# AdaLN block of a delta-rule mixer and a three-matrix FFN on eight cores: the last tile turned on TensorE, its last passes in halves, the plan of the order chosen among eight

## What is computed

```python
mod = (_silu(c) @ wmod).reshape(8, 6, 1, -1)
sa, ca, ga, sb, cb, gb = (mod[:, 0], ..., mod[:, 5])
ga, gb = (both with their sign kept and their size raised to at least 0.25)
h = _layernorm(x) * (1 + ca) + sa
x = x + ga * attn(h)
h = _layernorm(x) * (1 + cb) + sb
x = x + gb * jnp.tanh(h @ weight @ aux_weight1 @ aux_weight2 + bias)
# attn: q, k, v = silu(causal conv of 4 taps of x @ Wq, Wk, Wv), 4 heads of 256
#   o = chunkwise delta rule(l2norm q, l2norm k, v, beta), chunks of 32
#   mix = p0 * v + p1 * conv3(v) + p2 * conv31(v), p a softmax over three
#   o = rms_norm(g * o + (1 - g) * mix); return o @ Wo
```

## Time and profile before

| | |
|---|---|
| median of 3 timed runs | 774.94 us (773.45 to 778.86) |
| the profiled execution | 777.23 us |
| its span on the slowest core (core 5) | 775.7 us |
| spans of the eight cores | 760.5 to 775.7 us |
| busy: TensorE, VectorE, ScalarE, GpSimd | 706.0 (91%), 581.7 (75%), 419.6 (54%), 192.4 us (25%) |
| chain that ended last, by engine | TensorE 70%, DMA 14%, VectorE 5%, issue 4% |
| matmuls of TensorE | 5888 |

### The profile page before, as it was taken

How to read it: one execution, slowest core, us unless ns; L and a number is a source line. 1 busy time by engine, 2 the same in 40 slices (tenths; PEclk the granted TensorE clock), 3 DMA queues, 4 the chain that set the end, 5 groups by cost and what they waited for, 6 DMA issues and landing times.

```text
span 775.7 us, 17911 instructions; the slowest of 8 cores (760.5 to 775.7 us)
## 1 busy us (share of the span) xinstructions
PE 706.0 (91%) x5888; PEld 485.6 (63%) x5888; DVE 581.7 (75%) x1554; ACT 419.6 (54%) x915; POOL 192.4 (25%) x167
## 2 busy tenths in 40 slices
PE   3679997998897987899999999999999989999996
PEld 1234474576685876678778778788887844444432
DVE  3554755477879778887887798798798777787885
ACT  1132463466657655785766657686675632254422
POOL 1000000025406333462332242133234103040110
PEclk9999996699999999999999999999999999999999
DMA  8999898561453344335423505223249597829944
GB/s 225 320 321 320 252 279 182 183 90 56 75 70 106 47 89 114 45 69 86 94 42 58 122 15 83 80 73 97 71 55 174 155 193 189 238 62 239 216 88 150
DMA packets 121488, 105.15 MB, mean 136 GB/s; under 512 B 68926, under 2 KB 102261, under 8 KB 121014
## 3 DMA queue, kind: packets, MB, share of 16 engines
q1 hardware_dynamic: 98150, 89.29, 44.7%
q0 software_dynamic: 20944, 10.53, 11.5%
q10 hardware_dynamic: 2304, 4.20, 1.5%
HBM read 79.38 MB, written 18.89 MB: 127 GB/s over the span
## 4 chain that ended last, share of the span: by engine, by line
PE 70%; DMA 14%; DVE 5%; issue 4%; SPq 3%; ACT 2%; POOL 1%; ACTq 0%; DVEq 0%; POOLq 0%
PE ps L930 19%; PE ps L976 10%; PE ps L1613 7%; PE ps L1559 5%; DMA z_k<-w 3%; PE ps L1331 3%; PE ps L1295 2%; PE ps L705 2%; DMA w1t_sb<-wk 2%; PE ps L1227 2%; PE ps L1442 2%; PE ps L1421 2%; DMA w_d<-w_sb 2%; PE ps L1390 2%; PE ps L649 1%
## 5 line engine op out<-in xcount | busy, mean ns | idle before, releaser
L930 PE MATMUL ps<-h,wq_sb 128*128 128x256 bf16 x512 | 72.0, 288 | 3.4 <-DVE S L1450 3.0
L930 PE MATMUL ps<-h,wk_sb 128*128 128x256 bf16 x512 | 69.1, 276 | 1.3 <-ACT h L904 0.7
L930 PE MATMUL ps<-h,wv_sb 128*128 128x256 bf16 x512 | 65.9, 272 | 0.0
L930 PEld LDWEIGHTS ps<-h,wq_sb 128*128 128x128 bf16 x512 | 51.6, 103 | 16.9 <-issue 7.1
L1613 PE MATMUL ps<-wq_sb,h 128*128 128x512 bf16 x256 | 60.7, 380 | 0.3 <-DVE xf L1574 0.3
L1279 POOL TENSOR_SCALAR vbs<-vtm,gt 128x256 bf16<-128x256 bf16 x64 | 60.9, 963 | 0.0
L1559 PE MATMUL ps<-wk_sb,ofm 128*128 128x512 bf16 x256 | 57.4, 379 | 3.2 <-DMA ofm<-o_d 3.1
L1273 POOL TENSOR_TENSOR eb<-vtm 128x1024 bf16<-128x1024 bf16 x16 | 34.5, 2157 | 99.1 <-ACT vtm L391 37.8
L930 PEld LDWEIGHTS ps<-h,wk_sb 128*128 128x128 bf16 x512 | 48.7, 99 | 11.2 <-issue 3.2
L1118 DVE TENSOR_TENSOR E<-NN,cb_sb 128x512 bf16<-128x512 bf16 x112 | 48.9, 452 | 5.0 <-PE ps L1172 3.8
L807 PE MATMUL ps<-w1t_sb,w_sb 128*128 128x512 bf16 x128 | 34.2, 435 | 19.8 <-DVE w1t_sb L552 15.4
(11 more groups left out here) (240 smaller groups left out, 1821.5 us busy)
## 6 DMA issues: line engine op xcount, KB each, us to landing
xs<-x SPq DMA_DIRECT2D x16, 512.0 KB, 5.6
mst<-wmod POOLq DMA_DIRECT2D x16, 512.0 KB, 5.9
xf<-x SPq DMA_DIRECT2D x16, 512.0 KB, 4.6
out<-xf SPq DMA_DIRECT2D x16, 512.0 KB, 2.9
w1t_sb<-wk SPq DMA_DIRECT2D x8, 512.0 KB, 10.6
w1t_sb<-wq SPq DMA_DIRECT2D x8, 512.0 KB, 7.3
w1t_sb<-wv SPq DMA_DIRECT2D x8, 512.0 KB, 5.4
o_d<-ob ACTq DMA_DIRECT2D x16, 256.0 KB, 2.2
```

The costliest lines, as they stand in the source:

```text
L930: (lambda e, g=g: e.matmul(bk[:, 256 * i:256 * (i + 1)], wt[:, 2048 * p + 256 * g + 128 * i:2048 * p + 256 * g + 128 * (i + 1)], hv[:, 256 ...
```

## The change

Five edits.

- weave plans eight times, each time with the tails of the plan before. It keeps the tails that gave the plan whose last store ends first by the planner's own costs, and lays out all engines by them. These are the tails of the first plan, so the order used is the second plan; before it was the third.
- The planner's cost of an SP or ACT DMA is 480 ns for each DMA of a step and no longer 60 for the step; for POOL it is 600 for each.
- A Share gives banks only if `keep` more would still be free: two for most, one for ring_x, none for ring, ring_l and ring_r.
- The last tile's normed x is no longer turned by a DMA. Eight transposes on TensorE in two banks (new line L1620) and two casts into h2 replace it.
- The last tile's multiply, add and store (new lines L1670, L1672, L1675) work on two halves of 512 columns. For this th is posted half by half.

```diff
     def ready(self, n):
-        return self.pool.ready(n) if n <= self.cap else None
+        return self.pool.ready(n) if n <= self.cap and self.pool.ready(n + self.keep) is not None else None
...
-            return Step({eng: (emits, 600.0 if eng == "gpsimd" else 60.0)}, [t for t in after if t is not None],
+            return Step({eng: (emits, (600.0 if eng == "gpsimd" else 480.0) * len(emits))}, [t for t in after if t is not None],
...
-            tails = None
-            for turn in range(2):
-                tails = layout(None, None, tails).tails_of()
+            if not plan:
+                tails, found = None, []
+                for turn in range(8):
+                    trial = layout(None, None, tails)
+                    found.append((max(trial.board["out", n].at for n in range(NC)), turn, tails))
+                    tails = trial.tails_of()
+                plan.append(min(found)[2])
+            tails = plan[0]
...
+                    else:
+                        evs = []
+                        for half in range(2):
+                            mm = yield st("tensor", [t], lambda bk, half=half: [
+                                (lambda e, g=g: e.transpose(bview(bk)[:, 128 * (g % 4):128 * (g % 4 + 1)],
+                                                            xn2[n % 3][:, 128 * g:128 * (g + 1)], eye))
+                                for g in range(4 * half, 4 * half + 4)], 4 * mmw(128), ring=ring_o)
+                            ev = yield evac([mm] + fr, h2[n % 3][:, 512 * half:512 * (half + 1)],
+                                            bview(mm.banks[0])[:, 0:512], 512)
+                            ring_o.give(mm.banks[0], ev)
+                            evs.append(ev)
+                        post("h2", n, evs)
...
+                    for part in (slice(0, 1024),) if n < NC - 1 else (slice(0, 512), slice(512, 1024)):
+                        half_ths = []
+                        for half in range(part.start // 512, part.stop // 512):
+                            half_ths.append((yield Need(("th", n, half))))
+                        width = part.stop - part.start
+                        t3 = yield st("vector", half_ths + [rp], [lambda e: e.tensor_tensor(
+                            th[n % 2][:, part], th[n % 2][:, part], gb_rep[:, part], ALU.mult)], 1.15 * width)
+                        t4 = yield st("vector", [t3] + xts, [lambda e: e.tensor_tensor(
+                            x[:, part], x[:, part], th[n % 2][:, part], ALU.add)], 1.15 * width)
+                        t = yield dma("sync", s_out[n % NXF], [t4], [
+                            lambda e, n=n: e.dma_start(out_r[n, :, part], x[:, part])], 500.0 * width)
```

30 lines of the change are left out of this document (14 added, 16 removed).

## The result

The changed kernel takes 785.25 us (median of 13 runs, 778.93 to 825.87), the kernel before 775.6 beside it. The ratio is 1.0102, with a 95% interval of 1.0076 to 1.0127: about 8 us slower, where 2.3 us faster was predicted. The medians take in every run, the ratios only those in which the cores of one die did not run at a lower clock than the others. The profiled execution took 783.8 us, 1.45 us under the median.

A forecast was written before the change was run, and what follows sets the result against it. TensorE was taken as the bound, winnable only in idle and low-clock time. The terms -5.2 - 1.3 + 4.5 - 0.3 + 0 gave -2.3 us on the median of 774.9: 772.6 us, range 762 to 784.

The forecast's parts named there:

- What bounds the kernel: Whole kernel: TensorE is the bound, so a new order can win back only its idle time and time at low clock.
- Part 1, the gap at 116 us: TensorE gap before z_q's convolution shrinks from 4.0 to about 2.1 us and the half-clock spell goes: -5.2 us.
- My sign of full clock from 120 to 130 on every core: After the gap near 116 us: granted clock of 1.0 from 120 to 130 us on every core.
- Part 2, the hand-over: After v's last convolution, near 622 us: less TensorE waiting on ofm loads, -1.3 us, bounds 0 and -3.1.
- Part 3, the late gb_rep: Last stage: gb_rep lands 50.1 us after the last convolution and holds up TensorE; +4.5 us, bounds 0 and +13.
- the stall of 3.5 us in front of tile 3: Last product, second half of tile 3: TensorE stops 3.5 us for a PSUM bank held because gb_rep is late.
- the row store: Store of the last gb row ahead of gb_rep: given 2.9 us to land, the nearest row being out<-xf.
- Part 4, the tail: Last tile: TensorE resumes some 1.5 us later, halved passes and store win it back; sum -0.3 us, bounds -1.8 and +1.5.
- Part 5, the rest: Rest of the order, TensorE's 25.6 us idle from 150 to 400 us: taken as 0, bounds -10 and +5.6.
- third rival: Tiles 0 to 3 and x loads of tiles 6 to 9: late gb_rep breaks the slot chain, 783 to 787 us; chance 0.20.
- low-clock rival: Near 116 us: the gap of 2.1 us or L649's four-byte matmuls still bring low clock, 776 to 778 us; chance 0.12.
- clearly better: Low-clock spell goes on every core, two POOL multiplies meet VectorE work they do not hold: 760 to 767 us; chance 0.20.

The follow-up runs named there:

- e15: Changed kernel, order unchanged, with the four gb-row loads cut to an eighth and the gb matmuls and row passes behind them cut too; ratio 1.0017 to the kernel before.
- e9: Changed kernel, second plan, with the last block's first v convolution planned only once the four gb rows are; ratio 1.0294 to the kernel before.
- e1: Kernel before with only the last tile's two edits (turned on TensorE, last passes in halves), old planner and third plan; ratio 1.0005 to the kernel before.
- e6: Changed kernel with the shares' keep undone (keep=0), all else as changed; ratio 0.9863 to the kernel before.
- e14: Kernel before with only the 480 ns DMA cost and the second plan, no keep and no tail edits; ratio 0.9980 to the kernel before.
- e19: e14, order unchanged, with the gb load that POOL issues at 573 us cut to an eighth; ratio 0.9850 to the kernel before, three runs.

## Why the prediction was wrong, point by point

**What bounds the kernel**: right. What was won or lost is idle time on TensorE and matmuls that ran slower, in about equal parts on the mean core.

**Part 1, the gap at 116 us (-5.2)**: right in mechanism and place. z_q's convolution follows the projections without a wait, and the largest wait near there is 2.08 us on the eight cores (3.98 in the earlier trace rows). TensorE and VectorE on core 3:

```profile
118.59 1.03 PE L939 MATMUL ps<-h,wq_sb 128*128 128x256 bf16 x8
119.46 1.04 PE L985 MATMUL ps<-z_q,cdiag 128*128 128x256 bf16 x8
120.34 0.34 PE L1083 MATMUL ps<-cb_sb,sqb 128*128 128x1 bf16 x8
```

The clock on that core from 120 to 130 us is 0.98; half clock came later and shorter (0.51 from 130 to 140, a stretch that I had not named). My sign of full clock from 120 to 130 on every core failed on cores 1 and 4 (0.66 and 0.50). Over 112 to 150 us the clock was 0.64 to 0.91 on the eight cores (mean 0.82) and is 0.78 to 1.00 (mean 0.88). The first wv projections start at 140.7 us at the latest (148.06 in the earlier trace rows) and at 138.7 on the mean core (141.4 before). Where the last convolution ends, the slowest core was 7.3 us ahead, the mean core 2.9. The sum had one slip: a gap cut from 4.0 to 2.1 us with the same matmuls around it is 1.9 won and not 1.3. No run took this edit alone, so its worth in the total is read from the trace and not shown by an experiment.

**Part 2, the hand-over (-1.3)**: wrong in sign. The waits on ofm in sum are 5.2 us on core 3 (3.1 in the earlier trace rows), and 3.7 on the mean core against 1.7. The step that failed is that I counted the matmuls ahead of each wait and took the landing of the loads as fixed. It is not: in the new order a gb load lies beside them. I had the place of the gb groups in hand, in part 3, and used it for their matmuls and row stores only, not for the 512 KB loads that they need.

**Part 3, the late gb_rep (+4.5)**: right in when, wrong in what it does. SP's, VectorE's and TensorE's rows:

```profile
668.54 0.35 SPq L1544 DMA_DIRECT2D gb_rep<-row_d  x1
...
670.41 2.80 PE L1635 MATMUL ps<-wq_sb,h 128*128 128x512 bf16 x8
673.47 1.90 PE L1635 MATMUL ps<-wq_sb,h 128*128 128x512 bf16 x8
...
673.79 1.23 DVE L1670 TENSOR_TENSOR th<-th,gb_rep 128x1024 f32<-128x1024 f32 x1 [1.62 <-DMA gb_rep<-row_d]
```

gb_rep is used 58.9 us behind the last convolution (I had 50.1 for its landing), and the multiply waits for it. But TensorE, held up in the recurrence and on ofm, comes to these products later than I had reckoned, so the stall of 3.5 us in front of tile 3 is not there: L1635 runs on. The +4.5 was charged to a place that costs nothing. e15 shows that the work of the gb steps costs nothing, e9 that this order pays more when they are forced ahead. One term was sized badly: the row store, which I gave 2.9 us to land, is issued at 667.31, and gb_rep is issued 1.2 us behind it. What made gb_rep late is TensorE's own lateness: the last group for it starts 47.6 us behind the last convolution, and I had 39.1.

**Part 4, the tail (-0.3)**: right. Core 3:

```profile
771.31 0.62 PE L1620 MATMUL ps<-cb_sb,xn 128*128 128x128 bf16 x8
...
772.75 1.89 PE L1635 MATMUL ps<-wq_sb,h 128*128 128x512 bf16 x8 [0.82 <-ACT h L392]
...
778.69 0.69 DVE L1672 TENSOR_TENSOR xf<-xf,th 128x512 f32<-128x512 f32 x1
```

0.62 and 0.82 are lost (1.5 foreseen). Behind the last matmul 4.7 us are left and were 6.4, a gain of 1.7 (1.8 foreseen). e1 measured the sum as nothing.

**Part 5, the rest (0)**: this term failed, though the idle time from 150 to 400 us moved little (25.6 to 23.6 us on the slowest cores). It was the largest unknown and I gave it no sign and its bounds only from POOL's multiply. That one cost less than before: three of four held VectorE, for 3.05, 4.00 and 4.73 us, and TensorE behind them for 0.96, 2.74 and 3.26, where I had counted 10. The fourth held one of 8 columns (L1064) for 1.55, which takes about 0.16 elsewhere. As for the rule that I had cited from the Trainium skill ("SBUF — State Buffer", "Who interferes with whom"), the trace agrees for three of them, L1323, L1127 and L1064: they have two inputs in SBUF and end with the multiply or up to 0.6 us behind it. The one of 3.05 (L1264) reads a single tile and a column of scalars, and it stretched too. But the new loss was no compute instruction at all. It was the transposition at 350 us, 0.43%. The first wv matmul of a block shows it on the mean core: the new order is 8.5 us ahead at the fourth block (338.0 against 346.4) and 4.9 at the fifth (406.2 against 411.1). So the order had won something in this stretch, and the meeting took it back. I had looked at every engine's order and at SP's, and not at which transfer of POOL's queue is in the air when SP issues a transposition.

**The rivals.** The time, 785, lies in the interval of the third rival (783 to 787), and its mechanism did not happen: no store or load chain broke. A hit of that kind is worth nothing for the next kernel. The range ended at 784 because that rival was the only way to lose that I had priced. The low-clock rival was wrong; "clearly better" came true only where keep is taken out (e6, and e14 with one load cut, e19).

The sum as it came, on the slowest core and read from the traces: 7.3 us ahead at the last convolution, 13.4 behind after it, and 6.1 us more of span. On the mean core it is 2.9, 12.2 and 9.3.

## What to carry to other kernels

When a change moves instructions, list for each transfer that an engine waits for which other transfers are in flight beside it on any queue, in the old order and the new. The transpositions and the 2 MB load here were issued within 0.3 to 1.0 us of the load that they met, the store of o_d 4.3 us behind it, and twice such meetings decided 1.3%. This planner knows costs and not meetings, so measure a few of its orders and don't take the one that it likes best. To test such a suspicion, cut the data of one transfer and leave the order alone, with the same cut in the kernel before as the control. And a stage between two landmarks that gets longer is no loss until the landmark is known to have stayed.

## What the hardware did that I had not expected

A transposition by DMA (h<-xs, 256 KB, 3.0 to 4.1 us from issue to landing in the other pairs behind 200 us) took 9.4 to 12.0 us when a 512 KB load was issued on POOL's queue 0.5 us after the first of the pair. One of o_d took 9.8 to 12.4 us with such a load 0.3 us ahead, and 5.4 to 8.7 in the same place without it. The Trainium skill, "DMA: Bandwidth & Descriptors", section "Queues, rings and completion order", says that each DMA engine takes turns between the queues, a packet at a time. An estimate from that page and the 3.2 us of a pair alone: with turns of equal length the second transposition would take twice its time beside one other queue, 6.4 us, and three times beside two, 9.6. ScalarE's store of o_d, issued at 353.32, was such a second one. The measured 9.4 to 12.0 are near the larger figure and above it; whether the turns are of equal length no run here shows.

The issue itself can stretch too, but not by such a load alone. The third ofm issue on SP takes 1.7 to 3.6 us beside it and took 1.2 to 3.5 before, without it. Only the fourth, right behind, is longer: 3.3 to 5.0 against 2.2 to 3.5. A 512 KB load issued on POOL's queue 1.0 us ahead of a 2 MB load on SP's landed after 11.0 to 18.8 us, and after 5.8 to 8.5 where the 2 MB load had gone out eight us before. With the 512 KB cut to 64 KB (e19) the wait for it was gone. To be first by a microsecond does not help the smaller one.
